# The last row tile of the last group handed to ScalarE and GpSimd, and three rows of the last but one hidden tile ahead of the last

## The reference

```
q_emb = relu(cond @ W3 + b3)
h0 = relu(((64 * x + sum_over_64_rows(x)) * q_emb) @ W2 + b2)
h = square(relu(h0 @ ternary(W_fc).T))              # 2048 wide
hn = h * rsqrt(mean(square(h)) + eps)
out = x + hn @ ternary(W_proj).T
```

## Time and profile before

| | us |
|---|---|
| median of 3 runs | 311.33 (311.16 to 311.47) |
| the profiled execution, whole | 311.55 |
| its span in the profile | 309.8 |

### The profile page before, as it was taken

The page is one execution under the profiler, slowest core; times in us unless marked ns, Lnnn a source line. Parts: engine busy times, 40 slices in busy tenths (PEclk is TensorE's granted clock), DMA queues, the critical chain, the costliest instruction groups (busy, mean ns, idle before and its releaser), DMA issues.

```text
span 309.8 us, 3790 instructions
## 1 busy us (share of the span) xinstructions
PE 304.8 (98%) x1278; PEld 232.9 (75%) x1278; DVE 188.4 (61%) x310; ACT 191.3 (62%) x282; POOL 114.9 (37%) x106
## 2 busy tenths in 40 slices
PE   8999999999999999999999999999999999999994
PEld 8654545447888888888888888888888888888883
DVE  0679999996888778886257335952233483222335
ACT  1682666697999599976746444555554445555540
POOL 1035586645433323335333331253333314333330
PEclk9999999999999999999999999999999999999999
DMA  6994644342654043113004200340000033000003
GB/s 213 353 338 153 212 128 105 102 123 81 179 163 102 1 102 37 34 34 68 2 0 177 95 0 1 135 139 0 0 0 2 0 135 138 0 0 0 2 1 138
DMA packets 31332, 27.03 MB, mean 87 GB/s; under 512 B 18736, under 2 KB 20816, under 8 KB 31312
## 3 DMA queue, kind: packets, MB, share of 16 engines
q1 hardware_dynamic: 29936, 26.22, 28.5%
q10 hardware_dynamic: 1376, 0.56, 0.7%
HBM read 18.39 MB, written 4.19 MB: 73 GB/s over the span
## 4 chain that ended last, share of the span: by engine, by line
PE 95%; DVE 2%; ACT 1%; issue 1%; DVEq 0%
PE ps_acc L366 37%; PE ps_out L378 35%; PE ps_acc L350 18%; PE ps_out L337 2%; PE ps_out L328 1%; PE ps_acc L421 1%; DVE x_sb L580 1%; PE ps_x L435 1%; ACT x_t L673 0%; ACT x_t L670 0%; ACT wv_sb L676 0%; DVE y_hi L523 0%; DVE x_t L510 0%; DVE y_lo L525 0%; DVEq L113 0%
## 5 line engine op out<-in xcount | busy, mean ns | idle before, releaser
L261 POOL TENSOR_TENSOR wv_sb<-wv_sb 128x512 f32<-128x512 f32 x55 | 71.8, 1306 | 121.9 <-DVE y_lo L525 114.8
L378 PE MATMUL ps_out<-w_t,y_hi 128*128 128x512 f32 x256 | 100.1, 391 | 0.0
L366 PE MATMUL ps_acc<-h_hi,w_t 128*128 128x512 f32 x256 | 100.0, 391 | 0.0
L378 PE MATMUL ps_out<-w_t,y_lo 128*128 128x512 f32 x256 | 99.6, 389 | 0.0
L366 PE MATMUL ps_acc<-h_lo,w_t 128*128 128x512 f32 x256 | 99.6, 389 | 0.0
L523 DVE CAST y_hi<-x_t 128x512 fp32r<-128x512 f32 x64 | 33.0, 516 | 86.2 <-PE ps_out L378 71.6
L670 ACT ACTIVATE x_t<-ps_acc 128x512 f32<-128x512 f32 x64 | 37.9, 592 | 62.0 <-PE ps_acc L366 62.0
L350 PE MATMUL ps_acc<-x_t,wv_sb 128*128 128x512 f32 x128 | 56.3, 593 | 0.3 <-DVE x_t L510 0.3
L366 PEld LDWEIGHTS ps_acc<-h_lo,w_t 128*128 128x128 f32 x256 | 48.1, 188 | 10.2 <-issue 0.2
L366 PEld LDWEIGHTS ps_acc<-h_hi,w_t 128*128 128x128 f32 x256 | 48.1, 188 | 10.2 <-ACT h_f L665 0.2
L378 PEld LDWEIGHTS ps_out<-w_t,y_hi 128*128 128x128 f32 x256 | 48.1, 188 | 10.1 <-DVE y_lo L525 0.3
(11 more groups left out here) (57 smaller groups left out, 171.3 us busy)
## 6 DMA issues: line engine op xcount, KB each, us to landing
x_sb<-in_x_dram SPq DMA_DIRECT2D x5, 1024.0 KB, 5.7
raw<-in_L_ffn_W_fc_dram SPq DMA_DIRECT2D x8, 512.0 KB, 6.4
raw<-in_L_ffn_W_proj_dram SPq DMA_DIRECT2D x8, 512.0 KB, 4.3
out_dram<-x_sb SPq DMA_DIRECT2D x16, 256.0 KB, 2.1
x_odd<-in_x_dram SPq DMA_DIRECT2D x2, 1024.0 KB, 7.5
x_sb<-in_x_dram SPq DMA_DIRECT2D x4, 256.0 KB, 4.7
wv_sb<-in_L_cond_W_dram SPq DMA_DIRECT2D x4, 256.0 KB, 8.6
x_t<-in_L_cond_W_dram ACTq DMA_DIRECT2D x1, 512.0 KB, 5.0
```

What stands on the lines that cost most here:

```text
L261: engine.tensor_tensor(acc, acc, y_sq[:, v % SQ_RING, :], ALU.add).then_inc(sq_added, 1)
L366: last = pe.matmul(ps_acc[:, (UNITS + v) % ACC_RING, :], w_t[:, j, k * P:(k + 1) * P], part[:, k, g * BANK:(g + 1) * BANK], start=(k == 0 ...
L378: last = pe.matmul(ps_out[:, t, :], part[:, v % RING, t * P:(t + 1) * P], w, start=(opens(v) and part is y_hi), stop=(closes(v) and part i ...
```

## The change

Four things are changed, all at the end of the last stretch.

1. In `project_last_two`, before, tile 62 is projected on row tiles 0 and 1, then (after the wait for `split` of tile 63) tile 63 on 0 and 1, and then both on 2 and on 3. Now tile 62 is projected on 0, 1 and 2, then (after the same wait) tile 63 on 0, 1 and 2, and then both on 3. The number of matmuls is the same.
2. VectorE's `finish` leaves out row tile 0 for the last group.
3. ScalarE multiplies row tile 0 by `rstd` from PSUM into the SBUF buffer `row_0` (an ACTIVATE with function Copy and the `rstd` column as scale), after waits for `rstd_ready` and `tile_summed`. GpSimd then adds `row_0` to `x_res[:, 0, :]`.
4. Row tile 0 is stored by a DMA from ScalarE's queue after a wait for GpSimd. SP stores row tiles 1, 2 and 3.

```diff
             def project_last_two():
                 pe.wait_ge(split, TILES - 1)
-                project_tile(TILES - 2, 0)
-                project_tile(TILES - 2, 1)
+                for t in range(TT - 1):
+                    project_tile(TILES - 2, t)
                 pe.wait_ge(split, TILES)
-                project_tile(TILES - 1, 0)
-                project_tile(TILES - 1, 1)
-                for t in range(2, TT):
-                    project_tile(TILES - 2, t)
+                for t in range(TT - 1):
                     project_tile(TILES - 1, t)
+                project_tile(TILES - 2, 3)
+                project_tile(TILES - 1, 3)
...
-                for t in range(TT):
+                for t in range(1 if r == GROUPS else 0, TT):
                     dve.wait_ge(tile_summed, TT * r + t + 1)
...
             take_root(GROUPS)
 
+            act.wait_ge(rstd_ready, GROUPS)
+            act.wait_ge(tile_summed, TT * GROUPS + 1)
+            act.activation(row_0, ps_out[:, 0, :], ACT.Copy, scale=rstd[:, 0:1]).then_inc(row_scaled, 1)
+            act.wait_ge(row_added, 1)
+            act.dma_start(out_rows[STRETCHES[GROUPS][0], 0], x_res[:, 0, :]).then_inc(stored, 16)
...
+            pool.wait_ge(res_loaded, 16 * GROUPS)
+            pool.wait_ge(row_scaled, 1)
+            pool.tensor_tensor(x_res[:, 0, :], x_res[:, 0, :], row_0, ALU.add).then_inc(row_added, 1)
```

More of the change, by code:

```diff
@@ L165, in adaln_ffn @@
         partial = x1_t[:, 0]
+        row_0 = x1_t[:, 1, 0, :]
         relu_y = x1_t[:, 1, 0:RING, :]
@@ L230, in adaln_ffn @@
         finished = sem("finished")
+        row_scaled = sem("row_scaled")
+        row_added = sem("row_added")
         merged = sem("merged")
@@ L313, in _ @@
                     load_res(0)
-            for n in range(GROUPS):
+            for n in range(GROUPS - 1):
                 for t in range(TT):
@@ L320, in _ @@
                     sp.dma_start(out_rows[STRETCHES[n + 1][0], t], x_res[:, t, :]).then_inc(stored, 16)
-                if n + 1 < GROUPS:
-                    load_res(n + 1)
+                load_res(n + 1)
+            for t in range(1, TT):
+                sp.wait_ge(finished, TT * GROUPS + t)
+                sp.dma_start(out_rows[STRETCHES[GROUPS][0], t], x_res[:, t, :]).then_inc(stored, 16)
             sp.wait_ge(stored, 16 * TT * GROUPS)
```

## The result

| | us |
|---|---|
| before, median of 15 runs | 311.36 (311.16 to 311.81) |
| changed, median of 15 runs | 312.22 (311.55 to 312.83) |
| ratio changed / before | 1.0024, 95% interval 1.0018 to 1.0031 |
| changed, the profiled execution | 311.89, span 309.9 |

The changed kernel is slower by 0.24%, 0.86 us by the medians. The forecast was 311.8 us in a range of 311.0 to 312.1, with "within 0.2%" as the likeliest outcome. So the direction of the sum was right, its size was about half, and the median lies 0.1 us above the range.

What follows compares the result with a forecast made beforehand. TensorE bounds the program except its end, where TensorE, VectorE and DMA limits tie. The later first store adds 0.47 us to 311.33, giving 311.80 us, other parts having slack; range 311.0 to 312.1.

Steps and rivals of the forecast that it cites:

- three limits that tie: At the end: TensorE for the fourth row tile, VectorE's steps at 0.66 us, DMA engines at 0.695 us a store.
- the deciding term: The final stores: the first is issued at 305.19 instead of 304.72, so the last byte comes 0.47 us later.
- the last store's earlier issue: SP's store of row tile 3 is issued 0.14 to 0.24 us earlier, claimed to be worth nothing.
- The matmul order: Last 16 matmuls: the 0.10 us loss at the second wait goes; row tile 1 completes at 304.37 instead of 304.03.
- first-store term: At the final stores: the first store leaves 0.47 us later and the end of the data moves by +0.47 us.
- some 0.04 us of release: Delay from TensorE's completing row tile 1 at 304.37 to VectorE's first step on it at 304.41.
- ScalarE and GpSimd: Row tile 0's new way: scaling 0.67 us, add 1.29 us (1.68 at most), store issued at about 306.05, with slack.
- The 1.45 us behind the data: Landing and program end, from the last data at 308.35 to the span's end at 309.8, taken as unchanged.
- the 1.75 us outside the span: Time of the whole execution beyond its span, taken as unchanged: span 310.27, whole 312.02.
- Exclusion of VectorE and GpSimd: Rival: the GpSimd add and VectorE's steps on row tiles block each other, +1.14 us, 312.5 us; chance 0.14.
- A higher rate by two queues: At the final stores: two queues move 430 GB/s, only +0.13 us, 311.46 us; counted as the forecast's low end.

## Why the prediction was right or wrong, step by step

**The three limits that tie, and the deciding term: right.** The prediction put the loss on the first store, not on any engine. The run that put that store off, and the one that took bytes away, show it. It was also right that the last store's earlier issue (306.38 - 301.57 = 4.81 us behind the tail's start, against 4.98) is worth nothing.

**The matmul order: right.** The stall at the second wait is gone: the matmul behind it starts at 303.05, and the next at 303.29, 0.24 us later where it was 0.33. One figure was a slip: by the prediction's own counting the matmul behind the wait is the seventh, at 303.30 and not 303.08, and the trace has it there (1.48 us behind the tail's start by both). Nothing hangs on it.

**The size of the first-store term: 0.47 forecast, 0.60 measured.** The step that failed is "with some 0.04 us of release it starts at 304.41". The matmul that completes row tile 1 ends at 303.75 + 0.39 = 304.14 in the profile of after, and VectorE's first step starts at 304.29, 0.15 us behind it. The prediction names no row for its 0.04; in the earlier trace rows that is the step from the end of `rstd` (303.90) to the first L580 (303.94), where VectorE follows on its own instruction and doesn't sit waiting for TensorE. The profile of the order alone, where it does wait, has 0.15 as well. So 0.11 of the missing 0.13 us are this release. The store follows 0.77 us later, as forecast, and the transfer rate held: the mechanism was right and this term of its sum too small.

**ScalarE and GpSimd: right within 0.12 us.** The scaling took 0.69 us (0.67 forecast), the add 1.29, and the store was issued at 305.92, 4.35 behind the tail's start (4.23 forecast). All that had slack.

**The 1.45 us behind the data ("which I leave as they are") and the 1.75 us outside the span: wrong in two ways.** Outside the span the changed kernel takes 0.1 us more (1.93 against 1.82), which was in no term; its cause is open. Inside, the trailing engine is gone in the four profiles, and their tails are longer by 0.26 to 0.35 us only, where the stores were shifted by 0.6. A profiled run's sum is then 0.3 + 0.1 = 0.4 us, as the four profiled executions show against before (311.58 to 311.89 against 311.36, 0.4 in the mean). In the other group of runs the loss is about 1 us, and the median is of both. A likely reading is that there the fetch comes among the stores and the trailing engine is back: the version with one queue had it trailing in its profile, and its median is 0.85 us above before. But that profile is of another kernel, this is argued, not shown, and it makes 0.7 to 0.8 of the 1 us. So a median 0.1 us above the range is made of the release, of the 0.1 us outside the span and of the mix of the groups. And that the forecast missed by only 0.4 us is in part luck, because about 0.3 us were given back in part of the runs by an engine that no longer trails, of which it knew nothing.

**The rivals.** Exclusion of VectorE and GpSimd (312.5) did not occur: 0.66 us a step and an add of 1.29. The median of 312.2 lies between the forecast and that rival, and only the trace tells that it is the forecast's mechanism with a larger size. On this the Trainium skill ("SBUF — State Buffer", section "SBUF: two separate sides") was right: it has the exclusion for two SBUF inputs, and here, with one tile in PSUM and a `rstd` column in SBUF, the trace shows none. A higher rate by two queues did not occur either: 363 to 421 GB/s in full slices. The Trainium skill's other rule, that issuing from a second engine brings no bandwidth ("DMA: Bandwidth & Descriptors", section "Issuing engines are not separate DMA queues"), agrees with that and with the two runs on the queues.

**The range** took its upper end from the transfer rate and left out everything that is not a transfer. 0.13 us at the first store and 0.1 us outside the span would have moved its end to 312.3.

## What to carry to other kernels

When the last stores keep the DMA engines full, the transfers end at the moment of their first byte plus bytes over rate; ask of every edit there when the *first* store leaves, and give the earliest-finished tile to the engine that finishes it fastest. Relief of an engine is worth something only if it has work to do in that time: here VectorE exchanged 0.66 us of work for 0.64 us of wait. Two edits that each cost next to nothing can cost together what neither does, so cost them as a pair, at the step that both of them feed.

## What the runs showed of the hardware

- A VectorE instruction that sits waiting for a matmul starts 0.15 us behind that matmul's end in the record (304.14 to 304.29); ScalarE's starts 0.09 us behind (303.68 to 303.77).
- An 8 KB instruction fetch takes one of the 16 DMA engines for 0.3 to 0.5 us (3.9% to 6.7% of 16 engines in 0.5 us). In all ten profiles where it falls among the stores, one engine ends up to 0.5 us behind the others, seen as a row of slices at 23 GB/s, a sixteenth of the full rate.
- VectorE's SCALAR_TENSOR_TENSOR with one tile from PSUM, one from SBUF and a column as scalar isn't slowed by a GpSimd add of SBUF tiles beside it, nor is the add: 0.66 us a step and 1.29 us.
- Two stores of 128 KB, issued closely, took SP's queue 1.21 us, and with such pieces the rate fell below 240 GB/s in slices between. Four of 256 KB, of which the first two were issued one right behind the other, took it 0.33 to 0.44 us each, where 0.66 us apart they took 0.33.
- 0.1 us outside the span came and went with the way of one row tile, and with none of its pieces put on as extra work.
